# One preparation stage of a fused two-layer kernel: expert rows added by GpSimd, a TensorE turn, one ScalarE table set, and a moved addition

## The chip, the core and the metric

The kernel runs on one core of a Trainium2 chip. A core has five engines that run their own instruction queues: TensorE (PE in the profile; PEld is its weight load), VectorE (DVE), ScalarE (ACT), GpSimd (POOL) and SyncE (SP), which issues most DMAs. They meet only at semaphores. SBUF is the working memory, PSUM (here `bank`, eight banks of 512 columns) is what TensorE writes and what GpSimd doesn't use in this kernel. The metric is the device time of one execution in microseconds (us).

## What is computed

The reference is two layers over 2 sequences of 2048 tokens of width 256: gated linear attention with a 14-expert MLP, then a state-space layer (Mamba, 48 heads) with a 16-expert MLP. What stands between them is what this case is about:

```python
xn = _layernorm(x, axis=-1)
x = x + _L0_attn_ref(xn, ...) + _L0_ffn_ref(xn, ...)
xn = _layernorm(x, axis=-1)
x = x + _L1_attn_ref(xn, ...) + _L1_ffn_ref(xn, ...)
# _L0_ffn_ref: each token's result is the sum over its two chosen experts
# _L1_attn_ref: proj = _rms(xn) @ in_proj_w.T, split into z, xc, B, C, dt;
dt = jax.nn.softplus(dt + dt_bias)      # = max(z, 0) + log(1 + exp(-|z|))
# _L1_ffn_ref: softmax of x @ router_w, the two best experts of 16
```

## The kernel before

The program runs stages one after another, each in a block of its own with a barrier at its end: layer 0, layer 0's experts, `front`, layer 1's experts (`experts1`), and the state-space stage `ssm`, which is by far the longest. The change touches `front` alone, which lies from about 1062 to 1268.8 us of the profiled span.

`front` goes over G = 8 pieces of TS = 512 tokens (four of each sequence), features on the partitions, in beats k = 0 to 10. In beat k every engine works on up to three pieces: a = k (load, add, mean, variance), b = k-1 (normalise), c = k-2 (projections, routing, decay rates). Each engine's order within a beat is written out by hand, and `done(engine, name, g)` makes an engine wait until step `name` of piece g is over.

The steps that the prediction speaks of, with their lines in the profile:

- SP loads a piece of the running sum (`acc`, L1603) and of the expert rows (`ring`, L1607; two rows for each token, so two tiles side by side), and stores `acc` again (L1624, after `base`), the high and low parts of the projected features (L1626, L1627, after `f_lo`), and the decay rates of piece c (L1631 to L1633, semaphore `a_out`).
- `rows_turned(a)` on PE (L1648) multiplies both expert rows of each token by the identity into the same PSUM bank, which adds and turns them at once: 16 fp32 matmuls, 32 records. DVE adds the sum to `acc` (L1872, `acc_sum`), PE takes the `mean` (L1673), DVE subtracts it (`xc`, L1888), ACT squares it (L1808), PE takes the variance (L1679), ACT makes rstd by logarithm and exponential (L1774 to L1783).
- DVE makes `xn` (L1877) and `hm` (L1882, two instructions); POOL adds `xn` to `acc` (L1830, `base`); ACT rounds `hm` to the high part (L1804); DVE subtracts for the low part `f_lo` (L1925). `project` on PE (L64 to L66, 12 matmuls) uses both, then `tokens` (L1725), `mean`, `token_rows` (L1699), `turn` (L1708), `scores` (L1715).
- For piece c, ACT makes |z| (`absz`, L1766), exp (`ez`, L1768), later ln and exp; DVE makes `mx` = max(z, 0) (L1856) and the rest of softplus, a running sum (L1914), and the routing: small 128x64 operations after `f_lo` (L1929 to L1947), then `cb` (L1949).
- After beats 5 and 9 DVE computes where each token goes among the experts (`places`, 31 operations), for which PE first counts (`ranks`, L1734). In beats 6 to 9 POOL scatters tokens by indirect DMAs (L1839).

Of the kernel before, what the change touches and what calls it, by code (L numbers as in the profile page):

```python
# [9 lines left out]
ACT = mybir.ActivationFunctionType  # L10
ALU = mybir.AluOpType
AX = mybir.AxisListType

P = 128
# [17 lines left out]
HM, PH, NST = 48, 64, 128  # L32
# [1504 lines left out]
def front(nc, pool, bank, wbc, acc_dram, rows_out, sorted_dram, f_dram, a_drams, ea_drams, dec_dram, home, disp1, swdge,  # L1537
# [6 lines left out]
    with ExitStack() as own:  # L1544
        def sb(name, shape, dt=F32):
            return own.enter_context(nc.sbuf_tensor("fr_" + name, shape, dt))
# [5 lines left out]
        ring = sb("ring", [P, 2, NJ, 2, D])  # L1552
# [5 lines left out]
        f_hi, f_lo = sb("f_hi", [P, KD, TS], F32R), sb("f_lo", [P, KD, TS], F32R)  # L1558
        b_feat = sb("b_feat", [P, TS])
        q = sb("dt_q", [HM, 12, TS])  # L1560
        absz, ez, u, lnu, d, corr, ru, mx, dt, adt, a_log, rest = (q[:, i, :] for i in range(12))
# [4 lines left out]
        ph = Phase(nc, pool)  # L1566

        def done(eng, name, g, per=1):

            if g >= 0:  # L1570
                eng.wait_ge(ph[name], (g + 1) * per)

        def has(g):
            return 0 <= g < G
# [20 lines left out]
        with nc.Block(no_gpsimd_drain=True) as block:  # L1595
# [45 lines left out]
            def _(pe):  # L1641
                def rows_turned(a):
                    done(pe, "x_tok", a - 3)
                    pe.wait_ge(ph[f"in{a % 2}"], (a // 2 + 1) * 16)
                    for j in range(NJ):
                        for k in range(KD):
                            for c in range(2):
                                i = pe.matmul(bank[:, k, j * P:(j + 1) * P], ring[:, a % 2, j, c, k * P:(k + 1) * P], col("ident"),  # L1648
                                              start=c == 0, stop=c == 1)
                    i.then_inc(ph["turned"], 1)  # L1650

                def steps(c):
# [84 lines left out]
                for k in BEATS:  # L1737
                    a, c = k, k - 2
# [19 lines left out]

            @block.scalar
            def _(act):  # L1760
                act.activation(neg_a[:, 0:1], col("A_log")[0:HM], ACT.Exp).then_inc(ph["rate"], 1)
                for k in BEATS:
                    a, b, c = k, k - 1, k - 2
                    if has(c):
                        done(act, "dt_ps", c)
                        act.activation(absz, bank[0:HM, 6, :], ACT.Abs, bias=col("dt_bias")[0:HM]).then_inc(ph["absz"], 1)  # L1766
                        done(act, "absz", c)
                        act.activation(ez, absz, ACT.Exp, scale=-1.0).then_inc(ph["ez"], 1)  # L1768
                    if has(b):
# [52 lines left out]

            @block.gpsimd
            def _(pl):
                for k in BEATS:
                    b = k - 1
                    if has(b):
                        done(pl, "xn", b)
                        done(pl, "xc", b)
                        pl.tensor_tensor(acc[:, b % RA], acc[:, b % RA], xn[:, b % 2], ALU.add).then_inc(ph["base"], 1)  # L1830
                    if k in SCATTER:
                        done(pl, "place", 0, PLACE_OPS)
                        done(pl, "x_tok", NS - 1)
                        for n in range(*SCATTER[k]):
                            for i in range(2):
                                m = 2 * n + i
                                if m >= 4:
                                    pl.wait_ge(swdge[f"sent0{m % 4}"], m // 4 * 16)
                                pl.indirect_dma_start(sorted_dram[:], bass.IndirectOffsetOnAxis(ap=disp1["place"][:, i, n:n + 1], axis=0),  # L1839
                                                      x_all[:, n, :], None).then_inc(swdge[f"sent0{m % 4}"], 16)  # L1840

            @block.vector
            def _(dve):
# [7 lines left out]
                for k in BEATS:  # L1851
                    a, b, c = k, k - 1, k - 2
                    if has(c):
                        done(dve, "dt_ps", c)
                        done(dve, "absz", c)
                        dve.tensor_scalar(mx, bank[0:HM, 6, :], col("dt_bias")[0:HM], 0.0, ALU.add, ALU.max).then_inc(ph["mx"], 1)  # L1856
                        done(dve, "ez", c)
                        dve.tensor_scalar_add(u, ez, 1.0).then_inc(ph["u"], 1)
                        done(dve, "logits", c)
                        dve.tensor_copy(rt["lg"][:], bank[:, 3, 0:NJ * NE].rearrange("p (j e) -> p j e", j=NJ)).then_inc(ph["lg"], 1)  # L1860
                        done(dve, "u", c)
                        dve.tensor_scalar_add(d, u, -1.0).then_inc(ph["d"], 1)
                        done(dve, "lg", c)
                        dve.tensor_reduce(rt["m"][:, :, 0:1], rt["lg"][:], AX.X, ALU.max).then_inc(ph["rmax"], 1)
                        done(dve, "d", c)
                        dve.tensor_tensor(corr, ez, d, ALU.subtract).then_inc(ph["c"], 1)
                        done(dve, "rmax", c)
                        dve.tensor_tensor(rt["sh"][:], rt["lg"][:], wide(rt["m"][:, :, 0:1]), ALU.subtract).then_inc(ph["shifted"], 1)
# [1104 lines left out]
```

## Time and profile before

| | us |
|---|---|
| three runs | 3044.24, 3051.06, 3055.55 (median 3051.06) |
| the profiled execution: its time | 3077.26 |
| its span, first to last instruction | 3075.5 |
| `front` in it | 1062 to 1268.8 |

In the whole span PE is busy 88%, DVE 77%, ACT 69% and POOL 64%, but these are means over stages with different limits: in `front` POOL is busy for 59 us of 207, DVE for 161. A busy time is a time on the engine; what sets the end is read from who waits for whom in a beat. In the order of rows below, PE's fp32 matmuls count twice in the profile (two records each).

### The profile page before, as it was taken

How to read it: one execution, taken by the hardware profiler on the slowest of the kernel's cores; microseconds unless marked ns; L12 is line 12 of the kernel's file. 1: busy time of each engine (PE TensorE's matmuls, PEld its weight loads, DVE VectorE, ACT ScalarE, POOL GpSimd, SP SyncE). 2: the span in 40 equal slices, each digit the busy share in tenths (PEclk: the TensorE clock that was granted, in tenths of full speed). 3: DMA queues.
4: the chain of work that ended last, by engine and by line, in shares of the span. 5: the costliest groups of instructions: out<-in, count | busy, mean ns of one | idle time of the engine just before them, and what ended most of it. 6: DMA issues, size and time to landing. Idle time of an engine off the chain costs nothing. (4 is left out here: it accounts for less than half of the span.)

```text
span 3075.5 us, 58620 instructions
## 1 busy us (share of the span) xinstructions
PE 2698.2 (88%) x17318; PEld 2115.5 (69%) x17318; DVE 2381.1 (77%) x5972; ACT 2125.7 (69%) x4682; POOL 1977.7 (64%) x1697
## 2 busy tenths in 40 slices
PE   3698899888659888379799999999999999999997
PEld 2366666665549755267578888787787878878786
DVE  2466667665467679557599999999899999999996
ACT  3444554542255466346499999999899999999997
POOL 2322222223514313555489999999999999999998
PEclk8789998998879999589899999999999999999999
DMA  5455454554766644436778776666767666666673
GB/s 136 106 170 175 164 188 153 171 194 146 229 185 199 192 144 155 157 124 187 226 247 237 232 244 205 218 208 209 232 202 219 207 210 220 205 217 204 194 219 123
DMA packets 320436, 588.35 MB, mean 191 GB/s; under 512 B 47888, under 2 KB 138800, under 8 KB 319632
## 3 DMA queue, kind: packets, MB, share of 16 engines
q1 hardware_dynamic: 305776, 545.07, 57.1%
q0 software_dynamic: 14352, 39.54, 3.4%
q8 instruction: 149, 2.44, 0.3%
q14 instruction: 159, 1.30, 0.2%
HBM read 464.44 MB, written 124.17 MB: 191 GB/s over the span
## 5 line engine op out<-in xcount | busy, mean ns | idle before, releaser
L2689 POOL TENSOR_TENSOR mm<-mt,cb 128x512 f32<-128x512 f32 x384 | 490.4, 1301 | 56.5 <-ACT mt L2639 54.0
L2619 ACT ACTIVATE mt<-a_wide,a_tok 128x128 f32<-128x128 f32 x1536 | 487.2, 389 | 3.2 <-POOL mm L2689 2.5
L2772 DVE SCALAR_TENSOR_TENSOR cv<-bank,taps,cv 128x509 f32<-128x509 f32 (+2 forms) x576 | 429.4, 745 | 13.6
L64 PE MATMUL bank<-f,wi 128*128 128x512 f32 x768 | 321.5, 419 | 15.3 <-DMA wi<-ssm_wi_split 15.2
L65 PE MATMUL bank<-f,wi 128*128 128x512 f32 x768 | 304.6, 397 | 0.0
L66 PE MATMUL bank<-f,wi 128*128 128x512 f32 x768 | 304.6, 397 | 0.0
L2706 POOL TENSOR_TENSOR yz<-y,zs 128x512 f32<-128x512 f32 x192 | 249.1, 1298 | 15.0
L2695 POOL TENSOR_TENSOR y_lo<-yz,y_hi 128x512 fp32r<-128x512 f32 x192 | 246.9, 1286 | 5.4 <-ACT y_hi L2644 3.8
L2702 POOL TENSOR_TENSOR y<-t 128x512 f32<-128x512 f32 x192 | 246.8, 1285 | 0.0
L2716 POOL TENSOR_TENSOR y<-y,ys 128x512 f32<-128x512 f32 x184 | 238.0, 1293 | 0.0
L2512 PE MATMUL bank<-mm,x_tok 128*64 128x128 f32 x3072 | 225.8, 283 | 13.3 <-POOL mm L2689 13.2
L2512 PEld LDWEIGHTS bank<-mm,x_tok 128*64 128x64 f32 x3072 | 160.8, 136 | 102.8 <-issue 67.5
L2639 ACT ACTIVATE mt<-mt 128x512 f32<-128x512 f32 x384 | 221.5, 624 | 5.8
L2520 PE MATMUL bank<-xd,b_tok 128*128 128x128 f32 x1536 | 222.4, 288 | 0.0
L2520 PEld LDWEIGHTS bank<-xd,b_tok 128*128 128x128 f32 x1536 | 185.8, 191 | 32.9 <-issue 32.9
L2814 DVE SCALAR_TENSOR_TENSOR part<-part,dec,bank 128x64 f32<-128x64 f32 x768 | 181.6, 278 | 13.6
L957 POOL TENSOR_TENSOR l_s_out<-l_s_raw,l_s_out 128x768 fp32r<-128x768 f32 x33 | 61.5, 1863 | 189.5 <-ACT l_s_out L805 189.5
L64 PEld LDWEIGHTS bank<-f,wi 128*128 128x128 f32 x768 | 145.5, 189 | 42.9 <-DMA wi<-ssm_wi_split 16.0
L64 PE MATMUL bank<-y_hi,wo 128*128 128x512 f32 x384 | 170.8, 445 | 3.6 <-POOL y_lo L2695 3.5
L1389 POOL DMA_INDIRECT expert_scratch<-ex_y,ex_home x77 | 74.0, 961 | 150.6 <-ACT ex_y L1478 147.8
L66 PEld LDWEIGHTS bank<-f,wi 128*128 128x128 f32 x768 | 144.9, 189 | 35.5
L65 PEld LDWEIGHTS bank<-f,wi 128*128 128x128 f32 x768 | 145.9, 190 | 26.3
(476 smaller groups left out, 8073.6 us busy)
## 6 DMA issues: line engine op xcount, KB each, us to landing
wi<-ssm_wi_split SPq DMA_DIRECT2D x192, 512.0 KB
a_wide<-a_scratch SPq DMA_DIRECT2D x192, 512.0 KB
l_fw<-ffn_split SPq DMA_DIRECT2D x72, 768.0 KB
ea<-ea_scratch SPq DMA_DIRECT2D x384, 128.0 KB
wo<-ssm_wo_split SPq DMA_DIRECT2D x192, 256.0 KB, 3.9
sorted_scratch<-ex_zeros SPq DMA_DIRECT2D x96, 130.5 KB
ssm_wi_split<-l_s_out SPq DMA_DIRECT2D x24, 512.0 KB
ey_x<-sorted_scratch SPq DMA_DIRECT2D x94, 130.5 KB
```

Of the source, the lines that this page charges most:

```text
L64: pe.matmul(out, wh, xh, start=first, stop=False)
L65: pe.matmul(out, wh, xl, start=False, stop=False)
L66: return pe.matmul(out, wl, xh, start=False, stop=last)
L2512: i = pe.matmul(bank[h * PH:(h + 1) * PH, INTRA, chunk(j)], x_tok[:, j, h * PH:(h + 1) * PH], mm[:, h, chunk(j)], start=True, stop=True)
L2520: i = pe.matmul(bank[:, UPD, chunk(j)], b_tok[:, g // NCT * NJ + j, :], xd[:, j, :], start=True, stop=True)
L2619: i = act.activation(mt[:, h, chunk(j)], a_wide[:, g % R, h, chunk(j)], ACT.Relu, bias=a_tok[:, s * NJ + j, 2 * t + h:2 * t + h + 1], scal ...
L2689: pl.tensor_tensor(mm[:, :, ts], mt[:, :, ts], cb[:, js, :].rearrange("p j t -> p (j t)") .unsqueeze(1).broadcast_to([P, 2, TS // 2]), ALU ...
L2695: pl.tensor_tensor(y_lo[:], yz[:, g % 2], y_hi[:].bitcast(F32), ALU.subtract).then_inc(ph["y_lo"], 1)
L2702: pl.tensor_tensor(y[:], t1[:], t2[:, g % 2], ALU.add).then_inc(ph["y"], 1)
L2706: pl.tensor_tensor(yz[:, g % 2], y[:], zs[:, g % NS], ALU.mult).then_inc(ph["yz"], 1)
L2716: pl.tensor_tensor(y2[:], y2[:], ys[:], ALU.add).then_inc(ph["y2"], 1)
L2772: dve.scalar_tensor_tensor(cv[:, a:TS], bank[:, X, 0:TS - a], taps[:, t, k:k + 1], cv[:, a:TS], ALU.mult, ALU.add).then_inc(ph["tap"], 1)
```

## The change

Four edits, all in `front`:

1. POOL gets a new step `pair(a)`: when the expert rows of piece a have landed, it adds the second row of every token to the first, in place (128 x 4 x 256). `rows_turned` waits for it and only turns the sum: 8 transposes in place of 16 matmuls.
2. `mx` = max(z + bias, 0) goes from DVE to ACT (a Relu ahead of `ez`).
3. ACT loads once, at the start, one table set that has both the logarithm and the exponential.
4. POOL's addition `base` waits for `f_lo` too. In POOL's queue `pair(k + 1)` stands behind `base` of beat k and ahead of that beat's scatters.

```diff
@@ tensor
 def rows_turned(a):
     done(pe, "x_tok", a - 3)
-    pe.wait_ge(ph[f"in{a % 2}"], (a // 2 + 1) * 16)
+    done(pe, "pair", a)
     for j in range(NJ):
         for k in range(KD):
-            for c in range(2):
-                i = pe.matmul(bank[:, k, j * P:(j + 1) * P], ring[:, a % 2, j, c, k * P:(k + 1) * P], col("ident"),
-                              start=c == 0, stop=c == 1)
+            i = pe.transpose(bank[:, k, j * P:(j + 1) * P], ring[:, a % 2, j, 0, k * P:(k + 1) * P], col("ident"))
@@ scalar
+act.preload_act_table_set("natural_log_exp_and_others")
 act.activation(neg_a[:, 0:1], col("A_log")[0:HM], ACT.Exp).then_inc(ph["rate"], 1)
 ...
         act.activation(absz, bank[0:HM, 6, :], ACT.Abs, bias=col("dt_bias")[0:HM]).then_inc(ph["absz"], 1)
+        done(act, "dt", c - 1)
+        act.activation(mx, bank[0:HM, 6, :], ACT.Relu, bias=col("dt_bias")[0:HM]).then_inc(ph["mx"], 1)
@@ gpsimd
+def pair(a):
+    pl.wait_ge(ph[f"in{a % 2}"], (a // 2 + 1) * 16)
+    pl.tensor_tensor(ring[:, a % 2, :, 0, :], ring[:, a % 2, :, 0, :], ring[:, a % 2, :, 1, :], ALU.add).then_inc(ph["pair"], 1)
+
+pair(0)
 for k in BEATS:
     b = k - 1
     if has(b):
         done(pl, "xn", b)
         done(pl, "xc", b)
+        done(pl, "f_lo", b)
         pl.tensor_tensor(acc[:, b % RA], acc[:, b % RA], xn[:, b % 2], ALU.add).then_inc(ph["base"], 1)
+    if has(k + 1):
+        pair(k + 1)
@@ vector
-        done(dve, "dt_ps", c)
-        done(dve, "absz", c)
-        dve.tensor_scalar(mx, bank[0:HM, 6, :], col("dt_bias")[0:HM], 0.0, ALU.add, ALU.max).then_inc(ph["mx"], 1)
```

On GpSimd, from the start of `front`, before:

```order
L1823 UNCONDITIONAL_BRANCH
L1830 TENSOR_TENSOR fr_acc<-fr_acc,fr_xn 128x1024 x6
L1839 DMA sorted_scratch<-x_all,disp_place 12288x261 x8
L1830 TENSOR_TENSOR fr_acc<-fr_acc,fr_xn 128x1024
L1839 DMA sorted_scratch<-x_all,disp_place 12288x261 x8
```

and in the changed program, from the sixth beat on (L1828 is `pair`, L1837 is `base`, L1848 the scatter; lines below L1644 have shifted):

```order
L1837 TENSOR_TENSOR fr_acc<-fr_acc,fr_xn 128x1024
L1828 TENSOR_TENSOR fr_ring<-fr_ring 128x4x256
L1848 DMA sorted_scratch<-x_all,disp_place 12288x261 x8
L1837 TENSOR_TENSOR fr_acc<-fr_acc,fr_xn 128x1024
L1848 DMA sorted_scratch<-x_all,disp_place 12288x261 x8
```

Eight additions have become sixteen, and each `pair` stands directly behind a `base`.

On ScalarE, in one beat of the middle, before (`fr_dt_q` is the tile that holds all of softplus's rows, `fr_ln` the two rstd rows):

```order
L1766 ACTIVATE fr_dt_q<-bank,tab 48x512
L1768 ACTIVATE fr_dt_q<-fr_dt_q 48x512
L1774 ACT_TABLE_LOAD
L1774 ACTIVATE fr_ln<-bank,fr_small 128x512
L1775 ACTIVATE fr_ln<-bank,tab 128x512
L1778 ACTIVATE fr_dt_q<-fr_dt_q 48x512
L1781 ACT_TABLE_LOAD
L1781 ACTIVATE fr_ln<-fr_ln 128x512
```

and now:

```order
L1765 ACTIVATE fr_dt_q<-bank,tab 48x512
L1767 ACTIVATE fr_dt_q<-bank,tab 48x512
L1769 ACTIVATE fr_dt_q<-fr_dt_q 48x512
L1775 ACTIVATE fr_ln<-bank,fr_small 128x512
L1776 ACTIVATE fr_ln<-bank,tab 128x512
L1779 ACTIVATE fr_dt_q<-fr_dt_q 48x512
L1782 ACTIVATE fr_ln<-fr_ln 128x512
```

Both table loads are gone from the beat, and the Relu (L1767) has come in. The load that the whole program needs before the next stage's tanh stands there now (one), and one stands at the start of `front`.

On TensorE, the same beat's place of `rows_turned`, in the difference (L1648 before, L1647 now; L1657 and L1655 are `steps`, L1665 and L1663 `logits`):

```order
-L1657 MATMUL bank<-fr_hm,tab 48x512 x2
-L1665 MATMUL bank<-tab,fr_xn 128x16 x8
-L1648 MATMUL bank<-tab,fr_ring 128x128 x16
+L1655 MATMUL bank<-fr_hm,tab 48x512 x2
+L1663 MATMUL bank<-tab,fr_xn 128x16 x8
+L1647 MATMUL bank<-tab,fr_ring 128x128 x8
 L64 MATMUL bank<-fr_f_hi,fr_bc_hi 128x512
```

Its place in the queue is the same, ahead of `project` (L64).

## Rows read from the trace of the kernel before

**Rows 1.** Windows of three stretches: length, busy time (count) of PE, PEld, DVE, ACT, POOL; PE clock, DMA.
```profile
1136.70:1154.80 18.10, 16.86 (x102) 12.15 (x101) 17.48 (x46) 13.91 (x23) 2.80 (x1) 1.00 0.58 186
...
1173.00:1202.40 29.40, 24.09 (x108) 14.61 (x108) 26.99 (x77) 13.96 (x22) 9.24 (x7) 0.83 0.45 137
...
1238.60:1268.80 30.20, 12.38 (x55) 9.33 (x54) 20.89 (x82) 9.60 (x18) 12.66 (x12) 0.61 0.30 101
```

**Rows 2.** Timeline of beat 3, DVE and POOL: start us, us, engine, line, operation.
```profile
1136.70 0.15 DVE L1929 TENSOR_TENSOR fr_rt_m<-fr_rt_top 128x4 f32<-128x4 f32 x1
...
1137.26 0.22 DVE L1940 TENSOR_TENSOR fr_pick_all<-tab,fr_rt_idf 128x64 f32<-128x64 f32 x1
...
1141.11 1.23 DVE L1872 TENSOR_TENSOR fr_acc<-bank,fr_acc 128x1024 f32<-128x1024 f32 x1
...
1142.61 1.23 DVE L1877 TENSOR_TENSOR fr_xn<-fr_xc,fr_ln 128x1024 f32<-128x1024 f32 x1 [0.27 <-ACT fr_ln L1781]
...
1143.75 3.51 DVE L1882 SCALAR_TENSOR_TENSOR fr_hm<-fr_xc,tab,fr_ln 128x512 f32<-128x512 f32 x2
1143.91 2.80 POOL L1830 TENSOR_TENSOR fr_acc<-fr_acc,fr_xn 128x1024 f32<-128x1024 f32 x1 [15.34 <-DVE fr_xn L1877]
...
1147.39 1.22 DVE L1888 TENSOR_TENSOR fr_xc<-fr_acc,bank 128x1024 f32<-128x1024 f32 x1
...
1154.84 0.15 DVE L1929 TENSOR_TENSOR fr_rt_m<-fr_rt_top 128x4 f32<-128x4 f32 x1
```

**Rows 3.** The 16 instructions of L1882: shortest, median, longest in ns.
```profile
L1882 DVE SCALAR_TENSOR_TENSOR fr_hm<-fr_xc,tab,fr_ln x16: 744/1788/2851, 1087.0 to 1229.5; 128x512 f32<-128x512 f32 x16
```

**Rows 4.** Timeline in layer 0, DVE and POOL.
```profile
253.60 2.41 POOL L964 TENSOR_TENSOR l_base<-l_x,l_xn 128x1024 f32<-128x1024 f32 x1 [19.04 <-DMA acc_scratch<-l_base]
...
254.02 2.07 DVE L1068 SCALAR_TENSOR_TENSOR l_rt_bi<-l_rt_lg 128x56 f32<-128x56 f32 x1
255.92 2.09 POOL L933 TENSOR_TENSOR l_qb<-l_qe,tab 128x512 f32<-128x512 f32 x2
...
256.37 0.72 DVE L1073 TENSOR_TENSOR l_rt_sh<-l_rt_bi,l_rt_m 128x56 f32<-128x56 f32 x1
```

**Rows 5.** Timeline of beat 3, TensorE's matmuls.
```profile
1137.19 3.82 PE L1648 MATMUL bank<-tab,fr_ring 128*128 128x128 f32 x32
1140.76 0.48 PE L64 MATMUL bank<-fr_f_hi,fr_bc_hi 128*128 128x512 f32 x1
...
1143.70 0.69 PE L1725 MATMUL bank<-tab,fr_dt_q 48*128 48x48 f32 x8
1144.33 1.98 PE L1673 MATMUL bank<-fr_acc,tab 128*128 128x512 f32 x4
1146.15 1.04 PE L1699 MATMUL bank<-tab,fr_xn 128*128 128x128 f32 x8
```

**Rows 6.** Timeline of the first beats: a wait of DVE and one of TensorE.
```profile
1084.70 1.23 DVE L1872 TENSOR_TENSOR fr_acc<-bank,fr_acc 128x1024 f32<-128x1024 f32 x1 [6.81 <-PE bank L1648]
...
1092.96 3.78 PE L1679 MATMUL bank<-fr_sq,tab 128*128 128x512 f32 x4 [5.00 <-ACT fr_sq L1808]
```

**Rows 7.** Windows of 2 us around that wait; the granted clock is third from the end.
```profile
1090.00:1092.00 2.00, 0.00 (x0) 0.00 (x0) 1.87 (x3) 1.20 (x2) 0.00 (x0) 0.95 0.41 158
...
1098.00:1100.00 2.00, 2.00 (x8) 0.74 (x6) 0.00 (x0) 0.43 (x1) 0.00 (x0) 0.85 0.86 251
```

**Rows 8.** Groups by line in `front`: count, busy us, mean ns, idle before.
```profile
L1774 ACT ACT_TABLE_LOAD x8 | 10.3, 1283 | 0.1
...
L1856 DVE TENSOR_SCALAR fr_dt_q<-bank,tab 48x512 f32<-48x512 f32 x8 | 5.9, 736 | 7.4 <-ACT fr_dt_q L1766 7.4
```

**Rows 9.** Timeline: SP's store of `acc` in beat 3, and ScalarE in beat 9.
```profile
1146.74 0.57 SPq L1624 DMA_DIRECT2D acc_scratch<-fr_acc  x1
...
1247.27 1.28 ACT L1787 ACT_TABLE_LOAD   x1 [5.01 <-DMA dec_scratch<-fr_dt_ends]
```

## The prediction

> **What bounds the stage now.** The change lies in one stage, so I read the page for where the stage lies, then the windows by beat, then the timeline of one undisturbed beat, and last the waits. The windows show a beat of 18.1 us in which VectorE is busy 17.5 and TensorE 16.9, ScalarE 13.9, GpSimd 2.8 [rows 1]. The reader is to see that two engines are nearly full and GpSimd nearly empty. The timeline says which of the two sets the beat: VectorE has no wait longer than 0.27 us, and the same instruction, the first after `f_lo`, starts at 1136.70 and again at 1154.84 [rows 2]. The beat is 18.14 us and VectorE is its chain. I call the start of that instruction F and count from it: `acc_sum` at F+4.41, `xn` at F+5.91, `hm` at F+7.05, `xc` at F+10.69, next F at F+18.14. From `xc` to the next F is 7.45 us of VectorE work that no edit touches.
>
> Three beats (from the end of beat 2 to that of beat 5) are like this one. The first two beats fill the pipeline; beat 6's stretch holds `places` and is 29.4 us long; the last 30.2 us are a tail in which VectorE is busy 20.9 [rows 1].
>
> **What the removals are worth.** `hm` is two equal instructions. The shortest of the 16 takes 0.744 us and the longest 2.851, and in the timeline both together take 3.51 while GpSimd's 128x1024 addition runs [rows 2, 3]. So the second one stands still for 2.85 - 0.74 = 2.1 us per beat; with `base` gone from there, that comes off VectorE. `mx` is 0.74 us, of which 0.66 is the time until the next starts [rows 2, 8]. The two table loads per beat (1.28 us each [rows 8]) come off ScalarE, and a Relu of about 0.67 us comes on; in the middle beats they are worth at most the 0.27 us that VectorE waits [rows 2]. `rows_turned` falls from 3.57 us of TensorE (1137.19 to 1140.76) to about 0.9: `token_rows` is just such a set of 8 transposes and takes 1.04 with its tail [rows 5]. Taken alone, these give 2.1 + 0.66 + up to 0.27 = 3.0 us per beat.
>
> **What the additions cost.** GpSimd's addition of 128x1024 takes 2.41 us where nothing holds it up [rows 4]; the 2.80 in this stage holds a wait of about 0.35 for the first `hm` [rows 2]. I take 2.45 for `base` and the same for `pair`, whose layout is not in the trace; its bounds are 2.41 and 2.80. `base` can start when `f_lo` ends, F+0.1, and `pair(k+1)` stands right behind it: the two end at about F+2.65 and F+5.3. Only then may TensorE turn the rows that it turned at F+0.49 before. Behind `rows_turned` are queued `project`, `tokens` and `mean`, and VectorE's `xc` waits for `mean`. From rows 5: `project` 2.94 (1140.76 to 1143.70), `tokens` 0.63, `mean` 2.0. So `xc` can't start before F + 5.4 + 0.9 + 2.9 + 0.6 + 2.0 = F+11.9. The ring's load is no part of this: it is issued a beat ahead.
>
> VectorE has its own way to the same place. In layer 0, a 128x56 operation with both inputs in SBUF took 2.07 us because GpSimd's addition had begun 0.4 us before it, and the next such operation took 0.72 since GpSimd's following instruction had the way again; both end when GpSimd's does [rows 4]. Here the small routing operations stand exactly behind `f_lo`. The first 128x64 one (L1939) waits until F+2.65, the second (L1940, before at F+0.56) until F+5.3. From L1940 to `acc_sum` it was 3.85 us, less `mx` 3.19: `acc_sum` at F+8.5, `xn` F+9.6, `hm` F+10.8 to 12.1, `xc` F+12.1. Both ways meet at F+12: the two gains of edits 2 and 4 are paid back by the new waits, and the beat becomes 12.1 + 7.45 = 19.5, 1.4 us longer than before. The Trainium skill (page "SBUF — State Buffer", section "Who interferes with whom") states that a VectorE instruction with two SBUF inputs and a GpSimd instruction that reads SBUF exclude each other for a whole instruction, which speaks against putting two GpSimd additions ahead of such operations. Layer 0's rows agree with it; were it false here, TensorE's way would give 11.9 in place of 12.1, so the sum would hardly move.
>
> **TensorE's clock.** TensorE's work of a beat now ends (variance, `steps`, `logits`) near F+0.6, and it then waits until F+5.4, 4.8 us. In beat 1 it waited 5.00 us, the granted clock fell from full to half (2.4 to 1.2 GHz) inside that wait, the variance after it took 3.78 us where it takes 1.98 otherwise, and the clock was back at about 1098.6, 5.6 us after work began [rows 6, 7]. If that happens here, 1.2 to 2.9 us of the turn, `project` and `mean` are lost, and `xc` is at F+13.1 to 14.8: the beat is 20.5 to 22.2, which is 2.4 to 4.1 longer. I think that it mostly does and take +3.3 per beat (bounds +1.4 and +4.1).
>
> **The other stretches.**
> - First beats, up to `xc` of beat 2: nothing is queued before `pair` yet, so the gains stand. `hm` twice 2.1; `acc_sum` of beat 1 waits 6.81 us for `rows_turned` [rows 6], whose end comes up to 2.7 earlier, less a start that `pair(0)` delays by 2.45 at a cold clock: 0.7 to 2.7; beat 2 the same by the shorter turn and one table load, 1.6 to 2.5. Sum -6.5 to -9.4; I take -8.
> - Three middle beats: 3 x 3.3 = +9.9 (bounds +4.2 and +12.3).
> - The stretch with `places` (29.4 us [rows 1]): the routing result comes 4.7 us later (L1940's wait), and 0.66, 2.1 and 0.18 go: +1.8 (bounds +1 and +3).
> - Beat 7: as a middle beat but before with a wait of its own: +2 (0 to +2.6).
> - Beats 8 and 9: no `pair`, but SP stands in its queue for `base`, now 2.45 + 0.1 us past `f_lo`, and then for one more store (0.57 [rows 9]), ahead of the stores of the decay rates, for which ScalarE's L1787 and with it VectorE wait: in beat 9 for 5.01 us [rows 9]. 3.2 later each, less a table load of 1.28 and `hm`'s and `mx`'s time where they still count: +2.0 and +1.8 (together +1 to +6).
> - The next stage's tanh needs a table load of 1.28: 0 to +1.3, I take +0.6.
>
> Sum: -8 + 9.9 + 1.8 + 2 + 3.8 + 0.6 = **+10.1 us**. The profiled execution took 3077.26 (span 3075.5 and 1.8 around it) and would take 3087.4. It lies 0.9% above the median of the runs, so I carry the difference over: 3051.1 + 10.1 = 3061 us, 0.33% slower. A difference under 0.5% (15 us) is about what a measurement of this kernel can't tell from none.
>
> **Rivals.**
> 1. *Forecast*: new waits eat the gains; +1 to +15 us. For it: both ways to `xc` are sums of rows. Chance 0.62.
> 2. *Slower by over 0.5%*: one mechanism, the clock. It falls in every beat's wait for `pair` and stays low for all of 5.6 us and more: +4.1 in three beats, +2.6 in beat 7, +3 in the stretch with `places` whose count and projections are cold too, and with the tail at its upper bound -6.5 + 12.3 + 3 + 2.6 + 6 + 1.3 = +18.7, 3070 us. It decides from 3.9 us per beat on. For it: the wait of 4.8 is as long as the one that lost the clock in rows 6 and 7. Against: the early gains must be at their lower bound as well. Chance 0.27.
> 3. *Faster by over 0.5%*: the additions on GpSimd are hidden, as they would be if the pair were ready before F. Then 3.0 us per beat fall in four beats, 8 to 9 at the start, some 3 with `places`, and the tail stays: -12 - 9 - 3 = -24, 3027 us. It decides where `rows_turned` starts before F+2. Against: `pair(k+1)` stands behind `base` in GpSimd's queue, and `base` waits for `f_lo`. With the middle beats even and the rest at its best it would be -9.4 - 2 = -11, not enough. Chance 0.09.
> 4. *Nothing*: the four edits even out to within 1 us of zero; that is inside the forecast's range and has the remaining 0.02.
>
> The range reaches from the start's best with a clock that holds and a tail that is hidden (-9.4 + 4.2 + 1 + 0 - 4 = -8, 3043) to a little past rival 2 (3072). Chances: faster 0.09, within 0.5% 0.63, slower 0.28.
>
> **What the profile of the changed kernel would show.** Right: two GpSimd additions of about 2.45 us back to back behind each `f_lo`; `rows_turned` waiting for the second of them, some 4.8 us; both `hm` at 0.74; L1939 and L1940's successors up to 2.4 us long; middle beats of 19.5 to 22.2 us; granted clock under 1 in each of them; `a_out` waits in beats 8 and 9 3 us later. Wrong: a middle beat under 18.1, `hm` still at 2.8, small operations at 0.2 while GpSimd adds, or a full clock throughout, which alone would bring the sum down to about +3. The prediction falls if GpSimd's `pair` is much slower than 2.45 by its layout (each us more is 8 us), or if the first beats gain more than 9.

## The result and the profile after

| | kernel before | changed kernel |
|---|---|---|
| median of 20 runs each, us | 3050.21 (3041.62 to 3055.55) | 3059.95 (3048.93 to 3070.01) |
| profiled execution: time / span, us | 3077.26 / 3075.5 | 3057.08 / 3055.3 |
| `front` in it, us | 206.82 | 213.83 |

The ratio of the changed kernel to the one before is 1.0032, 95% interval 1.0023 to 1.0041: it is slower by 9.7 us (7.0 to 12.5). Prediction: +10.1, 3061.0. The two profiled executions stand the other way round; whole spans of single executions differ by more than the change is worth. So I compare the stage by itself, from SP's first load of the ring to SP's first load of the next stage: +7.0 us. I cut it at the starts F of the first VectorE instruction behind each `f_lo` (beat 9 has no `f_lo`, and ends at the start of that same instruction):

| piece | before | changed | difference | predicted |
|---|---|---|---|---|
| first beats, to the first F | 56.53 | 48.37 | -8.2 | -8 |
| three middle beats | 18.14, 18.14, 18.13 | 20.42, 20.45, 20.47 | +6.9 | +9.9 |
| stretch with `places` | 29.44 | 30.79 | +1.4 | +1.8 |
| beat 7 | 19.43 | 20.44 | +1.0 | +2 |
| beat 8 | 16.78 | 18.87 | +2.1 | +2.0 |
| beat 9 | 15.86 | 19.65 | +3.8 | +1.8 |
| rest of the stage | 14.37 | 14.37 | 0 | 0 |

The predicted column sums to +9.5; the other 0.6 was for a table load in the next stage. It is there (1.28 us at 1305.84, behind an instruction that ended just before it, where the kernel before has none); what it adds to the total was not measured.

The timeline of a middle beat of the changed kernel, VectorE, GpSimd and the matmuls that count, from one F (1124.35) to the next:

```profile
1124.35 0.15 DVE L1935 TENSOR_TENSOR fr_rt_m<-fr_rt_top 128x4 f32<-128x4 f32 x1
...
1124.59 2.34 POOL L1837 TENSOR_TENSOR fr_acc<-fr_acc,fr_xn 128x1024 f32<-128x1024 f32 x1 [15.78 <-DVE fr_f_lo L1931]
1124.63 2.33 DVE L1942 COPY x_all<-fr_rt_idf 128x8 f32<-128x8 f32 x1
1126.89 2.34 POOL L1828 TENSOR_TENSOR fr_ring<-fr_ring 128x1024 f32<-128x1024 f32 x1
1126.94 2.37 DVE L1945 TENSOR_TENSOR fr_one_all<-tab,fr_rt_idf 128x64 f32<-128x64 f32 x1
...
1129.37 1.94 PE L1647 MATMUL bank<-tab,fr_ring 128*128 128x128 f32 x8 [4.39 <-POOL fr_ring L1828]
1129.96 0.68 DVE L1955 TENSOR_TENSOR cb<-bank,tab 128x512 f32<-128x512 f32 x1
1130.97 0.78 PE L64 MATMUL bank<-fr_f_hi,fr_bc_hi 128*128 128x512 f32 x1
...
1132.22 1.21 DVE L1878 TENSOR_TENSOR fr_acc<-bank,fr_acc 128x1024 f32<-128x1024 f32 x1
...
1134.49 1.40 DVE L1888 SCALAR_TENSOR_TENSOR fr_hm<-fr_xc,tab,fr_ln 128x512 f32<-128x512 f32 x2
1135.32 1.98 PE L1671 MATMUL bank<-fr_acc,tab 128*128 128x512 f32 x4
...
1137.34 1.22 DVE L1894 TENSOR_TENSOR fr_xc<-fr_acc,bank 128x1024 f32<-128x1024 f32 x1 [1.46 <-PE bank L1671]
...
1144.80 0.15 DVE L1935 TENSOR_TENSOR fr_rt_m<-fr_rt_top 128x4 f32<-128x4 f32 x1
```

Read it in pairs. GpSimd's two additions stand back to back, and beside each stands one small VectorE operation that ends with it: a copy of 128x8 that takes 2.33 us, and the 128x64 operation that takes 2.37 (0.22 before [rows 2]). TensorE has waited 4.39 us for the second addition and then turns 8 blocks in 1.94 us. `hm`, 3.51 before, takes 1.40. `xc` waits 1.46 for the mean and starts at F+12.99; before it was F+10.69 [rows 2].

The instructions of three lines, shortest, median and longest in ns, where those of L1882 stood before [rows 3]:

```profile
L1888 DVE SCALAR_TENSOR_TENSOR fr_hm<-fr_xc,tab,fr_ln x16: 733/734/744, 1079.8 to 1224.3; 128x512 f32<-128x512 f32 x16
L1942 DVE COPY x_all<-fr_rt_idf x8: 168/2337/2345, 1104.2 to 1255.3; 128x8 f32<-128x8 f32 x8
L1945 DVE TENSOR_TENSOR fr_one_all<-tab,fr_rt_idf x8: 210/2366/2369, 1106.5 to 1255.5; 128x64 f32<-128x64 f32 x8
```

The hold of 2.1 us has left `hm` altogether and has come back twice, on operations whose own work is 0.2 us. Busy time hides that: in the windows of the changed kernel (columns as in rows 1) VectorE is now "busy" 18.9 us of a beat, more than before, because a held instruction counts as busy:

```profile
1124.35:1144.80 20.45, 15.79 (x78) 10.86 (x77) 18.89 (x46) 11.40 (x22) 4.64 (x2) 0.83 0.50 165
1165.27:1196.06 30.79, 22.14 (x90) 13.32 (x91) 28.50 (x77) 12.04 (x22) 4.64 (x2) 0.78 0.38 109
...
1126.00:1128.00 2.00, 0.00 (x0) 0.00 (x0) 2.00 (x3) 0.76 (x2) 2.00 (x2) 0.50 0.00 0
...
1130.00:1132.00 2.00, 2.00 (x10) 1.81 (x9) 2.00 (x7) 1.00 (x2) 0.00 (x0) 0.50 1.04 406
1132.00:1134.00 2.00, 2.00 (x9) 1.65 (x8) 2.00 (x4) 0.67 (x2) 0.00 (x0) 0.83 0.64 163
```

TensorE's clock is granted 0.83 on the mean of the beat where it was 1.00 [rows 1]; it is at half (1.2 GHz) from F+1.5, inside the wait, to F+8.3 (from windows of 0.5 us).

Last, ScalarE in beats 8 and 9, as the wait of 5.01 us stood in [rows 9], and in beat 9 SP's last store of the rates that it waits for:

```profile
1228.32 0.63 ACT L1788 ACTIVATE fr_dt_q<-fr_dt_q 48x512 f32<-48x512 f32 x1 [5.58 <-DMA dec_scratch<-fr_dt_ends]
...
1241.86 1.51 SPq L1633 DMA_DIRECT2D dec_scratch<-fr_dt_ends  x1
...
1249.11 0.63 ACT L1788 ACTIVATE fr_dt_q<-fr_dt_q 48x512 f32<-48x512 f32 x1 [8.54 <-DMA dec_scratch<-fr_dt_ends]
```

The same store and the same ScalarE instruction in the kernel before, where F was 1238.62 (it is 1235.37 now):

```profile
1241.65 1.10 SPq L1633 DMA_DIRECT2D dec_scratch<-fr_dt_ends  x1
...
1248.56 0.63 ACT L1787 ACTIVATE fr_dt_q<-fr_dt_q 48x512 f32<-48x512 f32 x1
```

The start of the store goes from F+3.03 to F+6.49, the instruction from F+9.94 to F+13.74.

### The profile page after: what moved, and what is told of

The parts are those of the page before. It is cut to its first block, busy times and chain, and to the rows that moved or that the text cites. A ratio compares the mean times of both kernels' runs of the same rounds, so it can differ in the third digit from the quotient of the medians.

```text
span 3055.3 us, 58220 instructions
## 1 busy us (share of the span) xinstructions
PE 2663.3 (87%) x17126; PEld 2085.5 (68%) x17126; DVE 2388.6 (78%) x5964; ACT 2105.8 (69%) x4674; POOL 1993.0 (65%) x1705
## 4 chain that ended last, share of the span: by engine, by line
POOL 35%; issue 10%; ACT 3%; DVE 1%; PE 1%; DMA 1%; POOLq 1%; SPq 0%; ACTq 0%; DVEq 0%
POOL mm L2695 8%; POOL y L2708 7%; POOL yz L2712 7%; POOL y L2722 6%; POOL y_lo L2701 6%; ACT mt L2625 1%; DVE cv L2778 1%; DMA wi<-ssm_wi_split 1%; POOLq L2371 1%; ACT mt L2645 0%; ACT ys L2639 0%; ACT L2660 0%; POOL first L2737 0%; DVE bank L2849 0%; PE bank L64 0%
## 5 line engine op out<-in xcount | busy, mean ns | idle before, releaser
L64 PE MATMUL bank<-f,wi 128*128 128x512 f32 x768 | 321.4, 419 | 15.2 <-DMA wi<-ssm_wi_split 15.2
L2518 PE MATMUL bank<-mm,x_tok 128*64 128x128 f32 x3072 | 226.3, 283 | 13.4 <-POOL mm L2695 13.3
L64 PE MATMUL bank<-y_hi,wo 128*128 128x512 f32 x384 | 171.6, 447 | 3.4 <-POOL y_lo L2701 3.4
L64 PEld LDWEIGHTS bank<-f,wi 128*128 128x128 f32 x768 | 145.5, 189 | 42.6 <-DMA wi<-ssm_wi_split 15.7
```

The costliest lines, as they stand in the source:

```text
L64: pe.matmul(out, wh, xh, start=first, stop=False)
L2518: i = pe.matmul(bank[h * PH:(h + 1) * PH, INTRA, chunk(j)], x_tok[:, j, h * PH:(h + 1) * PH], mm[:, h, chunk(j)], start=True, stop=True)
```

## The experiments

Twelve kernels were run, in three groups of four (the first four, the next four and the last four below), each group on a chip of its own, beside runs of the kernel before: medians 3052.49, 3077.06 and 3056.04. A ratio is always to the kernel before of its own group; e9 has 6 runs, the others 12. Because the ratios can hardly tell 5 us, each kernel's stage is given as well, cut as above. "Middle" is the three beats between the first F and `places`. What is left behind beat 9 is 14.4 us in most kernels, 13.4 to 13.5 in e7, e9, e10 and e11, and 16.1 in e6. How well a piece repeats can be seen in e10, which differs from the kernel before only in SP's order and ran on another chip: its pieces up to beat 8 agree within 0.03 us.

| kernel | edits in it | stage | first | middle | `places` | beats 7, 8, 9 | ratio (95%) |
|---|---|---|---|---|---|---|---|
| before | none | 206.8 | 56.5 | 18.1, 18.1, 18.1 | 29.4 | 19.4, 16.8, 15.9 | 1 |
| changed | 1 to 4 | 213.8 | 48.4 | 20.4, 20.5, 20.5 | 30.8 | 20.4, 18.9, 19.7 | 1.0032 (1.0023 to 1.0041) |
| e1_base_early | 1 to 3 | 207.0 | 55.4 | 18.7, 19.5, 19.9 | 29.6 | 16.9, 17.0, 15.7 | 0.9993 (0.9977 to 1.0009) |
| e2_no_pair | 2 to 4 | 211.4 | 53.9 | 18.3, 22.2, 17.4 | 28.6 | 19.1, 19.2, 18.4 | 1.0012 (0.9997 to 1.0026) |
| e3_tables_relu | 2, 3 | 201.2 | 58.8 | 17.8, 17.8, 17.8 | 27.2 | 16.9, 15.8, 14.8 | 0.9988 (0.9977 to 1.0) |
| e4_warm | 1 to 4, PE kept busy | 209.8 | 48.3 | 19.6, 19.6, 19.6 | 30.7 | 19.7, 19.3, 18.5 | 1.001 (0.9991 to 1.003) |
| e5_pair_first | 1 to 4, `pair` first | 216.6 | 51.7 | 21.6, 20.9, 18.9 | 32.0 | 19.0, 19.1, 19.0 | 1.0031 (1.0017 to 1.0046) |
| e6_rates_first | 1 to 4, SP's order | 204.8 | 50.0 | 20.3, 20.4, 20.4 | 30.8 | 20.5, 14.8, 11.7 | 0.9994 (0.9978 to 1.0011) |
| e7_base_behind_hm | 2, 3, `base` behind `hm` | 191.3 | 52.7 | 16.5, 17.1, 17.2 | 27.0 | 16.9, 15.9, 14.7 | 0.9962 (0.9944 to 0.998) |
| e8_edit4_alone | 4 | 213.7 | 51.6 | 18.8, 19.2, 18.3 | 29.5 | 20.7, 20.9, 20.4 | 1.0038 (1.0018 to 1.0059) |
| e9_hm_rates_first | as e7, SP's order | 186.6 | 52.7 | 16.5, 17.1, 17.1 | 27.1 | 16.9, 15.0, 10.8 | 0.9939 (0.9921 to 0.9956) |
| e10_rates_first_alone | none, SP's order | 200.9 | 56.5 | 18.1, 18.1, 18.1 | 29.4 | 19.4, 16.8, 10.9 | 0.9977 (0.9964 to 0.999) |
| e11_pair_behind_hm | 1 to 3, `base` behind `hm` | 201.1 | 51.6 | 18.9, 19.5, 19.9 | 29.8 | 16.9, 16.1, 14.9 | 0.9973 (0.996 to 0.9986) |
| e12_table_alone | 3 | 199.9 | 56.4 | 17.8, 17.8, 17.8 | 27.6 | 17.3, 16.1, 14.7 | 0.9983 (0.9968 to 0.9998) |

Theory A below is the prediction's: GpSimd's two additions stand in front of both ways to `xc`, TensorE's turn and VectorE's small operations. Theory B is named with each.

### Where the additions stand: e1_base_early, e2_no_pair

e1 is the changed kernel with `base` where it was before, behind `xn`:

```diff
                         done(pl, "xc", b)
-                        done(pl, "f_lo", b)
                         pl.tensor_tensor(acc[:, b % RA], acc[:, b % RA], xn[:, b % 2], ALU.add).then_inc(ph["base"], 1)
```

> Edits 1 to 3 without edit 4: base no longer waits for f_lo, all else as in the changed kernel. Theory A (the price is the place: two GpSimd additions behind f_lo, with the turn behind them): the pair can run as soon as its rows have landed, rows_turned starts at about F+0.5 again, the clock holds in the middle beats, but hm shows 2.8 us again and the pair, wherever it now falls, holds some two-SBUF operation of VectorE for up to 2.3 us; beat about 19.5, total about 3052. Theory B (the pair on GpSimd is what costs, wherever it stands): 3060 as the changed kernel, beat 20.4.

Measured: the stage is 7 us shorter than in the changed kernel, as theory A said, and even with the kernel before. Beats 7 to 9 are 16.9, 17.0 and 15.7 (changed: 20.4, 18.9, 19.7; before: 19.4, 16.8, 15.9). But the middle beats (18.7, 19.5, 19.9) are longer than before, and part of theory A was wrong: `hm` isn't held in them. Beat 4, VectorE, GpSimd and the first of `project`:

```profile
1134.17 0.77 PE L64 MATMUL bank<-fr_f_hi,fr_bc_hi 128*128 128x512 f32 x1 [2.77 <-DVE cb L1954]
1137.76 1.40 DVE L1887 SCALAR_TENSOR_TENSOR fr_hm<-fr_xc,tab,fr_ln 128x512 f32<-128x512 f32 x2
1137.91 3.47 POOL L1836 TENSOR_TENSOR fr_acc<-fr_acc,fr_xn 128x1024 f32<-128x1024 f32 x1 [9.91 <-DVE fr_xn L1882]
1141.92 1.22 DVE L1893 TENSOR_TENSOR fr_xc<-fr_acc,bank 128x1024 f32<-128x1024 f32 x1 [2.76 <-PE bank L1671]
1144.01 2.66 POOL L1828 TENSOR_TENSOR fr_ring<-fr_ring 128x1024 f32<-128x1024 f32 x1 [2.63 <-DMA fr_ring<-expert_scratch]
1144.49 2.73 DVE L1907 TENSOR_TENSOR fr_dt_q<-fr_dt_q 48x512 f32<-48x512 f32 x1
```

This time GpSimd's `base` is the one that waits (3.47 for 2.34) and `hm` takes its 1.40, though `base` starts 0.15 us behind `hm` as it did before (3.51 and 2.80 [rows 2]). `pair` waits for its rows and then holds a VectorE operation behind `xc` for 2.73 in place of 0.68. And `xc` starts at F+9.99 only, since TensorE had waited 2.77 us for `cb` and runs `project` at the half clock. The beat adds up: 9.99 + 7.45 + 2.05 = 19.5.

e2 keeps `base` behind `f_lo` and takes `pair` out; the turn is again the 16 matmuls of before, waiting only for the rows' load (edit 1 undone in `rows_turned`, `pair` removed from GpSimd).

> Edits 2 to 4 without edit 1: TensorE adds the expert rows by 16 matmuls as before, base stays behind f_lo. Theory A: no wait of the turn and no lost clock; base holds the routing operations for 2.3 us where it held hm for 2.1, so a middle beat is 17.2 to 17.9, the last beats lose 4 to 6 us by the late stores, total 3045 to 3051. Theory B (base behind f_lo is itself the cost): middle beats of 19 or more and a total of 3056 or more.

Measured: 211.4, and 3057.74 us in all, which lies in theory B's range and not in A's. The middle beats are 18.3, 22.2 and 17.4 where A said 17.2 to 17.9. The beat of 22.2 stands out. TensorE's rows ahead of it:

```profile
1130.67 1.04 PE L1699 MATMUL bank<-tab,fr_xn 128*128 128x128 f32 x8
1133.86 0.66 PE L1708 MATMUL bank<-tab,fr_b_feat 128*128 128x128 f32 x4 [2.15 <-ACT fr_b_feat L1801]
...
1136.23 3.78 PE L1679 MATMUL bank<-fr_sq,tab 128*128 128x512 f32 x4 [0.73 <-ACT fr_sq L1811]
```

The granted clock was 1.00 through the wait of 2.15 us, fell to half at about 1135.4, and was back at about 1142.2 (windows of 1 us): the variance takes 3.78 in place of 1.98, and the next `acc_sum` comes at F+9.45. The waits alone don't explain it. In beat 3 of e8 TensorE did the same with longer waits, and the clock stayed at 1.00:

```profile
1127.49 0.66 PE L1708 MATMUL bank<-tab,fr_b_feat 128*128 128x128 f32 x4 [2.62 <-ACT fr_b_feat L1798]
...
1129.86 1.98 PE L1679 MATMUL bank<-fr_sq,tab 128*128 128x512 f32 x4 [0.73 <-ACT fr_sq L1808]
```

The other two beats are 18.3 and 17.4, on the mean 0.3 us less than before: the held copy (2.35 for 0.17) costs what the free `hm` gives, and about what e12 below gives for the table is left. The tail (19.1, 19.2, 18.4) stays long without `pair`: that part belongs to `base`.

### What each removal gives: e3_tables_relu, e12_table_alone, e8_edit4_alone

e12 is the kernel before with one line more; e3 has the Relu as well; e8 is the kernel before with edit 4's wait alone.

```diff
             def _(act):
+                act.preload_act_table_set("natural_log_exp_and_others")
```
```diff
                         done(pl, "xc", b)
+                        done(pl, "f_lo", b)
```

> Edits 2 and 3 alone: one table set, and max(z, 0) on ScalarE. Theory A: VectorE sets the beat, so 0.66 + 0.27 us per beat go, beat 17.2; with 1.3 us per wait on a table load in the first and the last beats the total is 3040 to 3045. Rival: TensorE, busy 16.9 of 18.1, takes over at once and the beat stays above 17.8, total 3047 to 3050.

> Edit 3 alone on the kernel before: one table set. ScalarE's loads delay VectorE by 0.27 us in a middle beat and by more in the first beats and in beats 8 and 9; middle beats 17.8 to 17.9, stage 202 to 205 us against 206.8, that is most of the 5.6 us that edits 2 and 3 give together, since there VectorE's saved 0.66 us ended in a wait for TensorE. Rival (the Relu's move is what gave the 5.6): stage 206 or more.

> Edit 4 alone on the kernel before: base waits for f_lo. The block moves from hm (2.1 us) to the routing operations (2.3 us), so the middle beats stay within 0.5 us of 18.14; SyncE's stores come 3 us later, and beats 8 and 9 get 2 to 4 us longer each. Stage 209 to 213 us against 206.8, total about 3055. Rival (edit 4 helps by itself): stage under 206.

Measured: e3's middle beats are 17.77 us and its median 3047.25, which is the rival's side (17.8, 3047 to 3050) and not theory A's 17.2. e12's are 17.77 too: in the middle beats the table gives 0.36 us and the Relu's move nothing. The reason is a limit that I had not counted. VectorE's row of `acc_sum` in a middle beat of e3:

```profile
1143.12 1.23 DVE L1872 TENSOR_TENSOR fr_acc<-bank,fr_acc 128x1024 f32<-128x1024 f32 x1 [0.77 <-PE bank L1648]
```

What VectorE saves ahead of `acc_sum` ends in this wait for the 16-matmul turn: it starts at F+4.41 in before, e3 and e12 alike. In the kernel before the turn ended at 1141.01 (1137.19 + 3.82 [rows 5]) and `acc_sum` began at 1141.11 [rows 2], so both ways were nearly even there already. e12's stage, 199.9, is 2 us under what was expected.

From `places` on, e3's pieces are 1.1 us shorter than e12's: that is what the Relu's move gives. e3's stage is longer than e12's by 1.3 all the same, through its first beats (58.8 to 56.4). There the first turn took 6.46 us to e12's 5.37 and the variance of beat 0 3.68 to 1.98: TensorE at a lower clock, before any Relu had run. So a stage length can carry some 2 us of such chance from its first beats.

The table alone is worth 6.9 us of the stage: 1.1 in the middle beats, 1.8 with `places`, 3.9 in beats 7 to 9. Edit 4 alone costs 6.9: 4.9 less at the start (`hm` is free), +1.9 in the middle, +9.9 in beats 7 to 9. That is more than was expected: middle beats up to 1.1 us above 18.14 in place of 0.5, and 4.1 and 4.6 in beats 8 and 9 in place of 2 to 4.

### The clock: e4_warm

The changed kernel, with 16 multiplications of the identity by itself ahead of the wait for `pair`, in pieces 3 to 7 (WARM is 16); their results aren't used.

```diff
     done(pe, "x_tok", a - 3)
+    if a > 2:
+        for _ in range(WARM):
+            pe.matmul(bank[:, 0, 0:P], col("ident"), col("ident"), start=True, stop=True)
     done(pe, "pair", a)
```

> The changed kernel with 16 more matmuls (identity by identity, into the bank that the turn overwrites, results unused) on TensorE ahead of its wait for the pair, in pieces 3 to 7; they take some 3.7 us of a wait of 4.4 to 4.8. Theory A: the granted clock stays full there, the turn and project take 0.9 + 2.9 us instead of 5.3, and xc moves from F+13.0 to about F+11.9 at best; 4 to 6 us less than the changed kernel, 3054 to 3056. Rival (the clock costs nothing, since VectorE is late too): 3060 as the changed kernel or above.

Windows and TensorE's timeline of e4 in the same beat:

```profile
1131.00:1133.00 2.00, 2.00 (x20) 2.00 (x20) 2.00 (x3) 0.67 (x2) 2.00 (x2) 1.00 0.00 0
1133.00:1135.00 2.00, 1.34 (x12) 1.15 (x12) 1.90 (x6) 0.00 (x0) 1.17 (x1) 1.00 0.97 375
```
```profile
1134.22 1.09 PE L1651 MATMUL bank<-tab,fr_ring 128*128 128x128 f32 x8 [0.66 <-POOL fr_ring L1832]
1135.84 0.47 PE L65 MATMUL bank<-fr_f_hi,fr_bc_hi 128*128 128x512 f32 x1 [0.53 <-DVE cb L1959]
...
1139.40 1.98 PE L1675 MATMUL bank<-fr_acc,tab 128*128 128x512 f32 x4
```

The clock is 1.00 in all middle beats, the turn takes 1.09 instead of 1.94, and the beat falls from 20.4 to 19.6. The clock's share is 0.8 us a beat and 3.3 us of the stage up to the end of beat 7; beats 8 and 9, which have no extra matmuls, differ by another 0.7. On TensorE itself the half clock costs 1.3: from the turn's start to that of `project` 1.60 for 1.09, and `project` 3.72 for 2.94. With it gone, TensorE stops at a third gate: the first matmul of `project` waits 0.53 us for VectorE's `cb`, which reads the PSUM bank that `project` writes next, and `cb` stands in VectorE's queue behind the held operations. In the changed kernel the slower turn hid that wait. So the two ways to `xc` are not independent.

### The pair ahead of base: e5_pair_first

```diff
                     b = k - 1
+                    if has(k + 1):
+                        pair(k + 1)
                     if has(b):
                         done(pl, "xn", b)
...
-                    if has(k + 1):
-                        pair(k + 1)
```

> The changed kernel with pair(k+1) ahead of base in GpSimd's queue, so that it waits for its rows only. If the wait of the turn for two additions is the price, it is gone: acc_sum stands at about F+5 instead of F+7.9, the clock holds in the middle beats, VectorE pays one block of 2.3 us at the pair (wherever its rows land) and one at base; middle beats of 19 to 19.7, the stage about 209 instead of 213.8 us, total about 3055. If the block of VectorE by two additions is the whole price, the beat stays 20.4.

A miss. GpSimd's and TensorE's waits over the stage:

```profile
POOL fr_ring L1828 <- DMA fr_ring<-expert_scratch: 84.9, 8, 15.1
...
PE bank L64 <- DVE cb L1955: 18.9, 6, 4.9
```

The rows of the next piece land only at F+15.9 to F+17.6, so `pair` can't be early: it runs across the end of the beat, and holds a VectorE operation there. `acc_sum` comes at F+5.7 (7.9 in the changed kernel), but `project` now waits up to 4.9 us for `cb`, because `base` still holds VectorE behind `f_lo`, and `xc` starts at F+12.14 in beat 3. The end of that beat:

```profile
1127.30 2.34 POOL L1828 TENSOR_TENSOR fr_ring<-fr_ring 128x1024 f32<-128x1024 f32 x1 [13.35 <-DMA fr_ring<-expert_scratch]
1127.53 3.19 DVE L1920 TENSOR_TENSOR_SCAN fr_dt_q<-tab,fr_dt_q 48x512 f32<-48x512 f32 x1
```

The scan takes 3.19 where it takes 1.20 otherwise: 12.14 + 7.45 + 1.99 = 21.6. The next beat is 11.62 + 7.45 + 1.83 = 20.9; in the third `pair` falls past the end, and it is 11.43 + 7.45 = 18.9. The turn has been freed, the other way binds, and the hold by `pair` has only moved behind `xc`.

### SP's order: e6_rates_first, e10_rates_first_alone

SP stores the decay rates of piece c ahead of everything of piece b; e6 does it in the changed kernel, e10 in the kernel before.

```diff
-                    if has(b):
-                        done(sp, "base", b)
-                        sp.dma_start(acc_dram[bb, :, :, ts], acc[:, b % RA]).then_inc(ph[f"kept{b % RA}"], 16)
-                        done(sp, "f_lo", b)
...
                     if has(c):
...
+                    if has(b):
+                        done(sp, "f_lo", b)
...
+                        done(sp, "base", b)
+                        sp.dma_start(acc_dram[bb, :, :, ts], acc[:, b % RA]).then_inc(ph[f"kept{b % RA}"], 16)
```

> The changed kernel with SyncE's stores of a beat in another order: decay rates first, then the projected features, the running sum (which waits for base) last. If the late stores behind base are what lengthens the last beats, beats 8 and 9 lose 3 to 4 us and the wait of L1788 falls from 5.6 and 8.5 us to under 5; the middle beats keep 20.4. Stage 209 to 211 us, total about 3056. Rival (the last beats are long because of the scatter's DMAs on the same engines): no change, 3060.

> The kernel before with SyncE's stores of a beat with the decay rates first and nothing else. If the long last beats are a fault of the kernel before already (L1787 waited 5.01 us in beat 9), the stage falls from 206.8 to 201 to 204; if the order of the stores only matters once base is late, it stays 206 to 207.

ScalarE of e6 in beat 9, where it waited 8.54 us:

```profile
1236.82 0.63 ACT L1788 ACTIVATE fr_dt_q<-fr_dt_q 48x512 f32<-48x512 f32 x1 [1.57 <-DMA dec_scratch<-fr_dt_ends]
```

e6's stage is 204.8, better than either theory gave. Beats 8 and 9 lose 12.1 us (14.8 and 11.7); the first beats (+1.6) and the rest behind beat 9 (+1.7) give 3.3 back, for which I have no reason. e10's is 200.9, just under what was expected: beat 9 falls from 15.9 to 10.9, and the rest by another 0.9. So the rates stood badly in SP's queue before the change too; edit 4 made it worse, since SP stands for `base` ahead of them.

### A better place for GpSimd's addition: e7_base_behind_hm, e9_hm_rates_first, e11_pair_behind_hm

`base` waits for `hm` instead of `f_lo`. e7 has edits 2 and 3 with it, e9 also SP's order of e6, e11 also edit 1.

```diff
                         done(pl, "xc", b)
+                        done(pl, "hm", b, KD)
                         pl.tensor_tensor(acc[:, b % RA], acc[:, b % RA], xn[:, b % 2], ALU.add).then_inc(ph["base"], 1)
```

> Edits 2 and 3, no pair, and base waits for hm instead of f_lo, so that GpSimd's addition begins while VectorE does xc, which reads one operand from PSUM. If only two-SBUF operations are held, xc stays at 1.2 us, hm at 0.74, and only the operations behind xc are late by 1.1 us; against edits 2 and 3 alone (beat 17.77, stage 201.2) the beat is 16.8 to 17.2 and the stage about 197, total about 3041. Rival (TensorE, 16.9 us per beat, is already the bound): beat 17.5 or more, stage 200 or more.

> Base behind hm, edits 2 and 3, no pair, and SyncE's stores with the decay rates first. The parts should add up where the last beats still wait for the rates (ScalarE's L1790 waits 22.7 us in all without the new order): beats 8 and 9 go from 15.9 and 14.7 to about 14 and 11.7, the middle beats stay at 16.9 to 17.2; stage 185 to 188 us against 191.3, total 18 to 22 us below the kernel before. Rival (the earlier stores only move the wait to the projected features or the running sum): stage 190 or more.

> The changed kernel with base behind hm in place of f_lo, so edits 1 to 3 with the two additions in the middle of the beat: base during xc, then the pair at once or when its rows land. If the place of the additions was all, this is as good as base behind hm without the pair (stage 191.3). If the pair costs a block of its own wherever it stands, about 1 to 2.3 us per beat come on top, stage 197 to 204. Edits 1 to 3 with base behind xn had 207.0, edits 2 and 3 with base behind xn 201.2.

The timeline of e9, VectorE and GpSimd:

```profile
1114.82 1.41 DVE L1883 SCALAR_TENSOR_TENSOR fr_hm<-fr_xc,tab,fr_ln 128x512 f32<-128x512 f32 x2
1116.40 2.38 POOL L1834 TENSOR_TENSOR fr_acc<-fr_acc,fr_xn 128x1024 f32<-128x1024 f32 x1 [13.87 <-DVE fr_hm L1883]
1117.78 1.22 DVE L1889 TENSOR_TENSOR fr_xc<-fr_acc,bank 128x1024 f32<-128x1024 f32 x1 [1.56 <-PE bank L1673]
1118.92 0.68 DVE L1893 TENSOR_TENSOR fr_dt_q<-fr_dt_q 48x512 f32<-48x512 f32 x1
```

Here GpSimd's 2.38 us lie beside a VectorE that waits 1.56 us for the mean and then runs `xc`, which has one input in PSUM and takes its plain 1.22. In the middle beats nothing is held; in the stretch with `places` and in beat 7 the operation behind `xc` is, by about 1 us (1.83 and 1.62 for 0.68). Middle beats are 16.5 to 17.2; e7's first beats and tail were shorter than I expected too (191.3 in place of about 197). e9 came out as expected at 186.6 (beats 8 and 9: 15.0 and 10.8, for about 14 and 11.7) and is the fastest kernel of this study: 0.61% faster than before (0.9939, 0.9921 to 0.9956).

e11 adds `pair` to e7 and gives 9.8 us back, 7.5 of it in the middle beats. GpSimd's rows of it, and the VectorE operation beside the second:

```profile
1111.48 2.36 POOL L1837 TENSOR_TENSOR fr_acc<-fr_acc,fr_xn 128x1024 f32<-128x1024 f32 x1 [12.85 <-DVE fr_hm L1888]
...
1115.86 2.35 POOL L1828 TENSOR_TENSOR fr_ring<-fr_ring 128x1024 f32<-128x1024 f32 x1 [2.01 <-DMA fr_ring<-expert_scratch]
1115.89 2.87 DVE L1908 TENSOR_TENSOR fr_dt_q<-fr_dt_q 48x512 f32<-48x512 f32 x1
```

`base` has found its free place; `pair` waits for the rows and starts 2 us later, amid VectorE's SBUF work, where it holds an operation of 0.68 us for 2.87. The middle beats are e1's (18.9, 19.5, 19.9): one such hold each, wherever `base` stands.

## Why the prediction was right

**Total.** +10.1 us predicted, +9.7 measured (+7.0 to +12.5 by the interval), and +7.0 by the stage's rows. What lies between the 7.0 and the 9.7 I can't assign; single stage lengths can carry some 2 us of chance (e3), and the interval reaches down to 7.0. That the totals agree to 0.4 us is partly luck: in the rows the middle beats were 3.0 us over-sized and beat 7 by 1.0, beat 9 was 2.0 under-sized, and the 2.7 us outside the stage hide the rest.

**The gains ahead of the first F.** Right in size, -8.2 for -8. The split into terms is not shown: edit 4 alone gives 4.9 there (for `hm` I had 4.2), edit 3 alone 0.1, and edits 2 to 4 without `pair` 2.6.

**The middle beats** were the step that was mis-sized: +2.3 each, not +3.3. `xc` at F+12.99 lies just under the band given for a lost clock, F+13.1 to 14.8. The mechanism stands (wait of 4.39 us, clock at half in it), but the clock was back at F+8.3, 3.3 us after the turn began, where I had gone by the 5.6 us of a first beat [rows 6, 7]. So only the turn and the first of `project` ran cold: 1.3 us on TensorE, the low end of the 1.2 to 2.9, and 0.8 on the beat (e4), where I had taken about 1.9. e4's beat of 19.6 is the 19.5 worked out for a warm clock, but two errors cancel in it. The two additions were to end at F+5.3, while 0.1 and twice 2.45 make 5.0, and they ended at F+4.9; and the wait for `cb`, 0.53 in e4, was not in the sum.

**Who is held behind `f_lo`.** Right in time, wrong in name. I had the two-input L1939 as the first held operation; it was the copy two places ahead of it (L1942 after), with one input in SBUF, and L1939 (L1945 after) was the second. The rule that I had cited, of the Trainium skill (page "SBUF — State Buffer", section "Who interferes with whom"), holds here for the two-input operations (2.37 us against 0.21). The copy of 128x8 is held as long (2.33 against 0.17); the same section states that copies too can take the ports shared with GpSimd, in a mode that uses both pairs, and I had not drawn on that; that this copy ran in that mode no trace shows. Since both additions were waited out either way, the sum was not touched.

**A wait that I did not list.** `project` also waits for `cb`. In the changed kernel it is nearly even with the others, in e4 it costs 0.53, in e5 it decides.

**What edits 1 to 3 are worth.** I had 3.0 us a beat for the removals "taken alone", 2.1 of it for `hm`, which edit 4 frees. e3 and e12 show the table and the Relu at 0.36 together in a middle beat as long as TensorE's turn is the old one; e7 shows 16.5 to 17.2 once `hm` is free as well, 1.0 to 1.6 less than before. The shorter turn, 2.7 us by the prediction, is what would lift the limit at F+4.41, but e11 against e7 shows that with its addition on GpSimd it costs 9.8 us of stage on balance.

**The tail.** Beat 8 right (+2.1 for +2.0), beat 9 under-sized: +3.8 for +1.8. The mechanism was the one named, SP standing for `base` ahead of the rates, and its size too: the store comes 3.5 us later, for which I had 3.2, and the table load of 1.28 behind the wait is gone. What I lacked is that from store to release it then took 7.25 us (1241.86 to 1249.11) where it was 5.62 before (1241.65 to 1247.27): 3.46 + 1.63 - 1.29 = 3.8. A likely reason, not tested by itself, is the store of `acc`: its 512 KB were issued 6.8 us ahead of F before (1231.86) and now at F+2.6 (1237.98), directly ahead of the other stores, and at the 373 GB/s of the window 1240 to 1242 they are 1.4 us of transfer (an estimate). e6, where the rates go first, has beats 8 and 9 shorter by 12.1 us and the stage by 9.0. Beat 7 was over-sized (+1.0 for +2), as a middle beat was; `places` came within 0.4.

**Rivals.** The slower one (clock) had its mechanism but not its price: its 3.9 us per beat are 1.4 and 2.5 for the clock, of which 0.8 was measured. The faster one (additions hidden) falls by the 4.39 us wait and, put into practice as e5, by the rows that land at F+16. Not tried, and open: e9 without the Relu's move, why e2 lost its clock in one beat where e8 kept it, and why `base` waits for `hm` in e1 where `hm` waited for `base` before.

## What to carry to other kernels

Put a GpSimd operation on SBUF where VectorE waits or works from PSUM, not behind an engine's last big operation where small ones are queued: here the same 2.34 us addition cost 2.1 us beside `hm`, the same and a turn's wait behind `f_lo`, and nothing beside `xc` in the middle beats, where it ended before VectorE's next SBUF operation. A wait given to one instruction is paid by all that stands behind it on other queues too: `base` held SP's store and with it ScalarE two steps on. Ask of each edit which of the ways to the next gate it shortens; one that shortens a way that isn't last gives nothing (the Relu in the middle beats), and its cost is still paid (`pair`).

## What was unexpected of the hardware

- A VectorE copy between SBUF tiles with a single input, as small as 128x8, was held for a whole GpSimd addition: 2.33 us in the changed kernel and 2.35 in e8, 0.17 in e12.
- The waits alone didn't tell whether TensorE's clock falls: with waits of 2.15 and 0.73 us it went to half in one beat of e2 (variance 3.78 us), and with 2.62 and 0.73 it stayed at full in e8 (1.98). In the changed kernel's middle beats it went to half in each wait of 4.3 to 4.4, and with 16 matmuls ahead of a wait of 0.66 it stayed at 1.00 (e4).
- Either engine can be the one held: with `base` starting 0.15 us behind the start of `hm`, `hm` took 3.51 and `base` 2.80 in the kernel before, and 1.40 and 3.47 in e1.
- GpSimd's addition of 128x1024 took 2.34 us in both of its layouts, the strided one in place and the flat one, back to back without a gap. The eight in layer 0 of the kernel before took 2.343 us at the shortest and 2.392 in the middle, so the 2.41 of [rows 4] was no lower bound.
